# A macaron block on one core: the value matmuls moved to the ends of the second and third quarters, and the masking of the first choice moved from VectorE to GpSimd

## The reference

```python
x = x + 0.5 * ffn(layernorm(x))      # 16 heads of 64, 8 experts
x = x + attn(layernorm(x))           # linear attention, 16 heads of 8
x = x + 0.5 * ffn(layernorm(x))
```

```python
gate_v = einsum('btc,hec->bthe', x, Ws)
w, sel = top_k(gate_v, 2)
mix_v  = einsum('bthk,bthke->bthe', sigmoid(w), one_hot(sel, 8))
v      = einsum('bthe,bted->bhtd', mix_v, einsum('btc,edc->bted', x, Wv))
attn   = softmax(q k / 8) v
mask_o = one_hot(top_k(x Wd, 2)).sum()
res    = einsum('bthe,bthd,efd->bthf', mask_o, attn, Wo).sum(2)
```

## Time and profile before

| what | us |
|---|---|
| median of 3 runs (lowest, highest) | 2470.3 (2469.51, 2485.37) |
| the profiled execution's own time | 2470.45 |
| its span, first to last instruction | 2468.7 |
| PE busy in it | 2348.8 |
| ACT busy | 2083.6 |
| DVE busy | 1960.9 |
| POOL busy | 1136.0 |

### The profile page before, as it was taken

The page is one execution under the profiler, slowest core; times in us unless marked ns, Lnnn a source line. Parts: engine busy times, 40 slices in busy tenths (PEclk is TensorE's granted clock), DMA queues, the critical chain, the costliest instruction groups (busy, mean ns, idle before and its releaser), DMA issues.

```text
span 2468.7 us, 119467 instructions
## 1 busy us (share of the span) xinstructions
PE 2348.8 (95%) x49920; PEld 2165.5 (88%) x49920; DVE 1960.9 (79%) x3498; ACT 2083.6 (84%) x6373; POOL 1136.0 (46%) x1126
## 2 busy tenths in 40 slices
PE   3999999999999999999999999999999999999997
PEld 3888898989889898888989889899898989989897
DVE  4887877878888788888888788787887887888874
ACT  3988888888888888888888889888888888889896
POOL 3454544535445355354454444553453544544431
PEclk9999999999999999999999999999999999999999
DMA  4565555655656655566656556566665655565564
GB/s 129 160 162 149 150 158 150 160 152 158 170 150 163 163 157 155 156 162 165 158 157 165 149 156 167 165 163 155 169 159 154 170 157 157 157 167 155 160 173 107
DMA packets 519381, 388.09 MB, mean 157 GB/s; under 512 B 214080, under 2 KB 436160, under 8 KB 510656
## 3 DMA queue, kind: packets, MB, share of 16 engines
q1 hardware_dynamic: 518416, 379.60, 57.5%
q10 hardware_dynamic: 432, 0.85, 0.1%
HBM read 191.64 MB, written 188.74 MB: 154 GB/s over the span
## 4 chain that ended last, share of the span: by engine, by line
PE 82%; DVE 8%; ACT 5%; issue 4%; POOL 1%; DMA 1%; SPq 0%; ACTq 0%; DVEq 0%; POOLq 0%
PE psT L453 18%; PE psS L408 15%; PE psT L470 7%; PE psS L496 6%; PE psT L421 6%; PE psT L472 6%; PE psT L471 6%; PE psT L496 5%; PE psT L465 5%; ACT PB L767 4%; PE psT L435 3%; DVE NMAX L647 1%; DVE QK L706 1%; PE psT L502 1%; DVE ST L729 1%
## 5 line engine op out<-in xcount | busy, mean ns | idle before, releaser
L767 ACT ACTIVATE PB<-psS,NMAX 128x256 f32<-128x256 f32 x2048 | 943.5, 488 | 71.3 <-DVE NMAX L647 68.0
L453 PE MATMUL psT<-V,PT 128*64 128x64 f32 x16384 | 550.0, 224 | 42.9 <-issue 42.2
L453 PEld LDWEIGHTS psT<-V,PT 128*64 128x64 f32 x16384 | 508.7, 138 | 74.0 <-issue 48.8
L706 DVE TENSOR_TENSOR QK<-psT,QK 128x512 fp32r<-128x512 f32 x512 | 341.8, 688 | 205.0 <-ACT QK L776 202.6
L408 PE MATMUL psS<-QK 64*128 64x256 f32 x6144 | 480.4, 291 | 0.2
L767 ACT ACTIVATION_READ_ACCUMULATOR PB<-psS,NMAX 128x1 f32 x2048 | 453.3, 221 | 0.0
L408 PEld LDWEIGHTS psS<-QK 64*128 64x128 f32 x6144 | 404.5, 186 | 32.1 <-issue 29.5
L647 DVE TENSOR_REDUCE NMAX<-psS 128x2 f32<-128x512 f32 x512 | 328.6, 683 | 85.7 <-PE psS L408 84.8
L776 ACT ACTIVATE QK<-psT 128x512 fp32r<-128x512 f32 x512 | 298.1, 621 | 112.5 <-PE psT L472 98.1
L875 POOL TENSOR_TENSOR BT<-MT,diagv 128x1024 f32<-128x1024 f32 x128 | 305.9, 2390 | 136.1 <-DMA MT<-MIXd 136.1
L856 ACT ACTIVATE PT<-psS 128x512 f32<-128x512 f32 x512 | 280.1, 604 | 52.2 <-PE psS L496 48.4
(11 more groups left out here) (119 smaller groups left out, 4589.3 us busy)
## 6 DMA issues: line engine op xcount, KB each, us to landing
Vd<-VM SPq DMA_DIRECT2D x128, 512.0 KB, 3.9
V<-Vd SPq DMA_DIRECT2D x128, 512.0 KB, 5.2
AOd<-AO SPq DMA_DIRECT2D x256, 256.0 KB, 3.8
PJd<-PJ SPq DMA_DIRECT2D x64, 512.0 KB, 2.8
PR<-PJd SPq DMA_DIRECT2D x64, 512.0 KB, 4.0
MIXd<-MIX SPq DMA_DIRECT2D x64, 128.0 KB, 1.7
MT<-MIXd SPq DMA_DIRECT2D x64, 128.0 KB, 4.4
MASKd<-MASKR SPq DMA_DIRECT2D x64, 128.0 KB, 4.0
```

The costliest lines, as they stand in the source:

```text
L453: last = eng.matmul(M[64 * u:64 * u + 64, (t * NT + it) * DH:(t * NT + it + 1) * DH], PT[:, t, jt, cols], V[:, pm % 2, 4 * r + t, jt, :], ...
L706: eng.tensor_tensor(QK[:, 1, ab], bank("qk", m).rearrange("p (k t) -> p k t", k=2), QK[:, 0, ab].bitcast(F32), ALU.subtract).then_inc(free ...
L767: eng.activation(PB[:, ab, j, it, :], psS[:, ab, j, it, :], ACT.Exp, bias=NMAX[:, ab, j, it:it + 1], accum_out=SUM[:, p % 2, it, 4 * r + t ...
```

## The change

Three things move, and one is rewritten.

1. `values` half 0 goes from the third quarter, behind `scores`, to the end of the second, just ahead of the turns; half 1 goes from the fourth quarter to the end of the third. With them their places in the list of items move, and with these the banks of nearly every item of the second, third and fourth quarters. ACT's copies to VM stay in the third and fourth quarters, but now stand ahead of the quarter's exponentials and not between its two halves.
2. In the third quarter `project` goes ahead of the turning of XN and AXN (`xturn`, `attn_x`, `attn_gram`) on PE, and the rounding and the subtraction likewise on ACT and DVE.
3. GM is no longer made by one DVE instruction at the end of the second quarter. POOL makes it at the start of its third quarter in two instructions, with a semaphore between them.
4. On DVE `largest(1)` moves behind the copies to OT and stands right ahead of the two subtractions.

```diff
@@ items_of @@
-            if r == 2 and runs(p + 1):
-                items += [("values", p + 1, 0, a) for a in range(2)]
-            if r == 3 and runs(p + 1):
-                items += [("values", p + 1, 1, a) for a in range(2)]
...
             if r == 2 and runs(p - 1):
                 items += [("expand", p - 1, b) for b in range(2)]
+            if works(n + 1):
+                items += [("qk", 2 * n + 2), ("qk", 2 * n + 3)]
             if r == 2:
...
-            if works(n + 1):
-                items += [("qk", 2 * n + 2), ("qk", 2 * n + 3)]
...
+            if r in (1, 2) and runs(p + 1):
+                items += [("values", p + 1, r - 1, a) for a in range(2)]
             if works(n):
                 items += [("turn", n, t) for t in (0, 1)]
@@ tensor_program @@
-                if r == 2 and runs(p + 1):
-                    values(p + 1, 0)
-                if r == 3 and runs(p + 1):
-                    values(p + 1, 1)
...
+                if r in (1, 2) and runs(p + 1):
+                    values(p + 1, r - 1)
                 if works(n):
                     turn(n, 1)
                     turn(n, 0)
@@ vector_program @@
-                if r == 2 and runs(q):
-                    eng.wait_ge(s_pick, at + 6)
-                    largest(1, GM[:, :, :])
...
+                if r == 2 and runs(q):
+                    eng.wait_ge(s_pick, at + 6)
+                    largest(1, GM[:, :, :])
                 if works(n + 1):
...
-                if r == 1 and runs(q):
-                    eng.wait_ge(s_pick, at + 5)
-                    eng.scalar_tensor_tensor(GM[:, :, :], F1[:, :, :], LOWEST, GS[:, :, :], ALU.mult, ALU.add).then_inc(s_pick)
@@ scalar_program @@
-                if works(n):
-                    exponentials(n, 0)
                 if r == 2 and runs(p + 1):
                     copy_values(p + 1, 0)
                 if r == 3 and runs(p + 1):
                     copy_values(p + 1, 1)
                 if works(n):
+                    exponentials(n, 0)
+                if works(n):
                     exponentials(n, 1)
+                if works(n + 1):
+                    rounded(n)
@@ pool_program @@
+            def without_first(q):
+
+                eng.wait_ge(s_pick, PICKS * q + 5)
+                eng.tensor_scalar(FW[:, :, :], F1[:, :, :], LOWEST, None, ALU.mult).then_inc(s_low)
+                eng.wait_ge(s_low, q + 1)
+                eng.tensor_tensor(GM[:, :, :], FW[:, :, :], GS[:, :, :], ALU.add).then_inc(s_pick)
...
+                if r == 2 and runs(p + 2):
+                    without_first(p + 2)
```

More of the change, by code:

```diff
@@ L217, in macaron_kernel @@
         s_turned = semaphore("s_turned")
+        s_low = semaphore("s_low")
         s_copied = [semaphore(f"s_copied{i}") for i in range(2)]
@@ L520, in tensor_program @@
                     expand(p - 1, 1)
+                if works(n + 1):
+                    project(2 * n + 2)
+                    project(2 * n + 3)
                 if r == 2 and runs(p + 3):
@@ L536, in tensor_program @@
                     last.then_inc(full("attn_gram", q))
-                if works(n + 1):
-                    project(2 * n + 2)
-                    project(2 * n + 3)
                 if r in (0, 1) and runs(p + 2):
@@ L697, in vector_program @@
                         eng.tensor_copy(OT[:, :, 64 * b:64 * b + 64], bank("expand", p - 1, b).rearrange("p (e k) -> p e k", e=E)).then_inc(freed("expand", p - 1, b))
-                if r == 2 and runs(p + 3):
-                    dst = XT[:, (p + 3) % 4]
-                    eng.wait_ge(s_xhi, p + 4)
-                    eng.tensor_tensor(dst[:, 1, :], bank("xturn", p + 3)[:, 0:T], dst[:, 0, :].bitcast(F32), ALU.subtract).then_inc(freed("xturn", p + 3))
+                if r == 2 and runs(q):
+                    eng.wait_ge(s_pick, at + 6)
+                    largest(1, GM[:, :, :])
                 if works(n + 1):
@@ L706, in vector_program @@
                         eng.tensor_tensor(QK[:, 1, ab], bank("qk", m).rearrange("p (k t) -> p k t", k=2), QK[:, 0, ab].bitcast(F32), ALU.subtract).then_inc(freed("qk", m))
+                if r == 2 and runs(p + 3):
+                    dst = XT[:, (p + 3) % 4]
+                    eng.wait_ge(s_xhi, p + 4)
+                    eng.tensor_tensor(dst[:, 1, :], bank("xturn", p + 3)[:, 0:T], dst[:, 0, :].bitcast(F32), ALU.subtract).then_inc(freed("xturn", p + 3))
                 if r == 2 and runs(q):
@@ L818, in scalar_program @@
                     eng.activation(GRAM[:, :], bank("attn_gram", q)[:, 0:C + 1], ACT.Copy).then_inc(freed("attn_gram", q))
-                if works(n + 1):
-                    rounded(n)
                 if r in (0, 1) and runs(p + 2):
```

## The result

The changed kernel takes 2624.49 us (median of 4 runs, 2622.77 to 2628.17) against 2473.19 us (2469.51 to 2485.37) of the kernel before beside it: ratio 1.0595, 95% interval 1.0559 to 1.0631. It is slower by 6%. Its profiled execution took 2623.25 us, of which the span is 2621.4, at a granted clock of 0.990; that is 152.8 us over the profiled execution before.

What follows compares the result with a forecast made beforehand. PE bounds the third quarter, ACT and DVE the fourth. Even passes +2.3 us, odd +3.2, mean 2.75 over some 60 of 64 passes is +165, less 30 of issue losses: +135 on 2470.45, 2605 us, range 2525 to 2660.

Steps and rivals of the forecast that it cites:

- Second quarter: End of second quarter: values half 0 adds 1.09 us in even passes, 1.52 in odd, where it waits for the second subtraction.
- Product waits for VM: Third quarter: product takes the bank of values half 0, so PE waits 0.54 us for ACT's first VM copy every pass.
- Even third quarter: End of even third quarters: values half 1 waits for DVE's XT until about 9.75 us; quarter 11.86 against 10.34, taken as +1.4.
- GM on POOL: POOL, third quarter: two GM instructions take about 2.3 us (1.1 to 4.4), hidden in even passes with 0.45 us margin.
- Odd third quarter: End of odd third quarters: values half 1 waits for POOL's BT until 9.3 us; quarter 11.4 against 9.57, +1.9 us.
- Fourth quarter: Fourth quarter: ACT and DVE bound it, so PE's loss of 1.09 us of values saves only 0.2 us.
- DVE without GM: DVE, end of second quarter: 111.9 us of busy time goes, 1748 ns each, with nothing more gained.
- Issue losses: PE at product: of 42.2 us lost to issue, 30 taken as gone, since each such product has a wait before it.
- POOL decided: Rival: a slower one-input GM instruction on POOL delays BT, 2646 us at 2.0 us, 2717 at 3.2; chance 0.12 (above 2650).
- The fourth quarter gave back: Rival: the fourth quarter shrinks by 0.9 us more because PE had fed ACT's chain late, 2551 us; chance 0.13.
- issue is the true bound: Rival: instruction feeding of PE paces the quarters, so the 42.2 us are won and new waits cost nothing, 2428 us; chance 0.08.
- The moves did not cancel: Rival that they cancel: values change quarters at no price and GM is hidden, 2470 us; chance 0.05 (within 1%).

Runs made afterwards that it cites:

- the last two of ACT's order: Changed kernel with turning and BT order undone, GM on DVE: both VM copies ahead of all PT copies, 2524.24 us; only half 1's ahead, half 0's between, 2493.5 us.

## Why the prediction was right

2605 us was predicted, 2624.49 measured, inside the range, and most waits were found where the walk had put them. By its steps:

1. *Second quarter.* +1.09 and +1.52 predicted. Passes 32 and 33 took 9.98 and 11.65 us, +1.16 and +1.59 on the same passes before. In the odd one values start at 1403.30, 0.10 behind the end of the second subtraction (1401.92 + 1.28); the trace puts the wait down to issue, but it is the bank.
2. *Product waits for VM.* 0.54 predicted, 0.48 by the starts (2.34 behind the scores, where 1.86 would do), of which the trace shows 0.41 as idle.
3. *Even third quarter.* Values at 9.75 predicted, 9.69 measured, for DVE's XT as named; 11.80 against 11.86. The run with the turning ahead confirmed both the cause and what is late next, BT at 9.3.
4. *GM on POOL.* The two-input instruction took 1169 ns (1.1 predicted), the one-input one 1503 ns (1.1 predicted, inside the bounds). Together 2.7 instead of 2.3 us. It stayed hidden in the even typical pass, as MB, two instructions ahead of it, had become 0.2 us shorter each with GM away from DVE (1959 against 2164 ns in the mean). The Trainium skill's GPSIMD Engine Reference, section 3.1, has rates by which, as an estimate, these two would take 1.11 and 0.77 us; the trace agrees with the first within 6% and is at twice the second, so its figure for a best-case body does not hold for this operand. That GM would cost nothing outside the typical pass was wrong: it cost 8 us alone and about 20 with the moves, and in the profiled executions half of it or more stands ahead of pass 6.
5. *Odd third quarter.* RSTD at 4.2, BT's end at 9.3 predicted; 4.20 and 9.27 measured. The quarter takes 11.63 (11.4 predicted): values start 0.25 behind BT's end.
6. *Fourth quarter.* Bounded by ACT and DVE, 9.03 predicted, 8.97 measured. The run with VM copied early and the last two of ACT's order show it directly. In the mean the quarter fell by 0.92; step 8 has why.
7. *DVE without GM.* Its busy time fell by 92.4 us and brought nothing, as predicted.
8. *Issue losses.* I took 30 us off, because `product` would lose them behind a wait. At `product` they did go (42.2 to 2.8). The sum of all lines with "issue" fell by 8 us only, but that count takes in waits for DVE's subtraction, most of them new. Without the matmuls that wait for a semaphore the losses fell from 44.0 to 13.0 us, by 31. The passes say the same: 32 and 33, which had no such loss, grew by 2.34 and 3.38 us, 2.86 in the mean, and the mean pass by 2.28, so 0.58 us a pass were not paid; and in passes 6 to 49 these losses fell from 0.77 to 0.20 us a pass. Most of them had stood in the fourth quarters (0.56 us a pass before, 0.02 after). The size is thus right. The reason given for it, a wait ahead of each `product`, is argued: with half 0 alone moved the fourth quarters had no such wait, and `product` lost 13 us in them where it had lost 33.

The sum: 2.86 us a pass where the prediction had 2.75, less 0.58 where it had 0.5, makes 137 us in 60 passes against 135. The measured 152.8 (profiled executions) holds 16 us more. Passes 4 to 63 took 139.8 of it, 2.33 each; the other 12.9 are there by the beginning of pass 4 (it starts at 210.1 us against 197.2). The prediction had left four passes out of its 64 as lacking a neighbour, and they are not free. That is the term that was too small. Of the 12.9 us 3.0 stand ahead of pass 0, and no term of the sum had them: there POOL's two instructions for GM, 1.5 and 1.2 us, stand twice on the chain that ended last. The six kernels with GM on POOL all begin pass 0 at 57.3 to 58.5 us, the eight without at 53.3 to 54.4. Passes 4 and 5 paid 11.0 us together, more than twice the mean.

The rivals: POOL decided less than its price list said, 1503 ns instead of 2 or 3 us. The fourth quarter gave back 0.27 us of its 1.09 in typical passes. In the mean it gave back 0.92, near to what this rival had, but 0.55 of that are the issue losses of step 8; with the VM copies elsewhere the typical quarter gave 0.82. That issue is the true bound is refuted by the time: 31 us of issue losses went and the kernel became 6% slower, with waits for BT and VM of 112 us in sum where 10 were before. The moves did not cancel.

## What to carry to other kernels

Moving work from the beginning of one stage to the end of the one before gains nothing when the stage is as long as a chain of other engines; it turns the time of the mover into waiting, and costs its full length where it goes. Walk each stage of a typical pass to the end and note, for the moved instruction, the latest of its inputs and of the releases of its bank: four numbers so found (2.40, 9.3, 9.3 and 9.75 us) measured 2.34, 9.12, 9.27 and 9.69 here. Look for the idle time of the off-path engine that would take the copy that the move requires, and put the copy there: that order, not the move, was worth 37 us. Walk the first passes too, where an instruction that the steady state hides can stand on the chain. And before a wait is called an issue loss, look at what the other engines end just ahead of it: 35 of 38 such waits of values were waits for a bank.

## What the runs showed of the hardware that was not expected

A DVE instruction with both inputs in SBUF is held up by a two-input instruction that runs on POOL. Timelines of the kernel before (GM on DVE beside MB on POOL, odd pass) and of the one after (ST on DVE beside BT on POOL). Before:

```profile
1320.84 2.28 DVE L713 SCALAR_TENSOR_TENSOR GM<-F,GS 128x512 f32<-128x512 bf16 x1
...
1320.61 1.96 POOL L881 TENSOR_TENSOR MB<-MASKT,diago 128x1024 f32<-128x1024 f32 x1
```

After:

```profile
1394.01 2.36 DVE L723 TENSOR_TENSOR ST<-SV,S 128x128 f32<-128x128 f32 x1
...
1393.80 2.42 POOL L869 TENSOR_TENSOR BT<-MT,diagv 128x1024 f32<-128x1024 f32 x1 [4.05 <-DMA MT<-MIXd]
```

Both DVE instructions end a fixed time behind POOL's, GM 0.55 us and ST 0.15 us, and so do the others of their kind. In the kernel before, 61 of the 64 GM began while such a POOL instruction ran and ended 545 to 550 ns behind it, taking 1411 to 2374 ns; the other three took 676 to 691. Of ST, after, 12 of 32 took 2353 to 2529 ns so, the other 20 took 291 to 293. POOL in turn pays: of the 64 second MB of a pair in the kernel before, the 59 that came while GM was running took 2398 to 2418 ns, the other five 1950 to 1961. With GM away from DVE the mean of all MB falls from 2164 to 1959 ns, and it is back at 2167 with GM returned. Where one input is in PSUM it does not show: the 97 QK subtractions of the kernel before that began beside such a POOL instruction took 674 to 694 ns.

A one-input instruction of POOL on bf16 (FW, 512 elements, 1503 ns) took longer than a two-input one of the same length with an f32 output (GM, 1169 ns).
